# Two PSUM banks for the scores and four for everything else, with a new table of places

## What is computed

```python
# layer 0: group norm, 8 heads of 32 channels, projection, residual
h = group_norm(x) * gn_w + gn_b
q, k, v = split(qkv_w @ h + qkv_b)                  # per head 32 x 1024
w = softmax((q * scale).T @ (k * scale), axis=-1)   # 64 score matrices of 1024 x 1024
x = x + proj_w @ (w @ v) + proj_b
# layer 1: one head, queries and keys of 32 channels, values of 256, residual
energy = (Wq @ x).T @ (Wk @ x)
x = gamma * (softmax(energy) @ (Wv @ x)) + x
```

## Time and profile before

| | |
|---|---|
| median of 3 runs | 1619.43 us (1619.39 to 1620.1) |
| the profiled execution | 1615.41 us |
| its span, first to last instruction | 1613.5 us |
| TensorE busy | 1500.4 us, 93% |
| GpSimd (POOL) busy | 1199.0 us, 74% |
| VectorE (DVE) busy | 1132.3 us, 70% |
| ScalarE (ACT) busy | 752.1 us, 47% |
| mean granted TensorE clock | 0.954 |

### The profile page before, as it was taken

The page is one execution under the profiler, slowest core; times in us unless marked ns, Lnnn a source line. Parts: engine busy times, 40 slices in busy tenths (PEclk is TensorE's granted clock), DMA queues, the critical chain, the costliest instruction groups (busy, mean ns, idle before and its releaser), DMA issues.

```text
span 1613.5 us, 25511 instructions
## 1 busy us (share of the span) xinstructions
PE 1500.4 (93%) x7120; PEld 897.8 (56%) x7120; DVE 1132.3 (70%) x1916; ACT 752.1 (47%) x1377; POOL 1199.0 (74%) x560
## 2 busy tenths in 40 slices
PE   4889798999999999999999999999999999999968
PEld 1454354558545774558555674457555584556437
DVE  3776668877687677877688777877788777684243
ACT  2046354653546444653546445554546535563412
POOL 3069887895779777895889877796878958797804
PEclk9689889999999999999999999999999999999979
DMA  4040304030411214030220314020140304000100
GB/s 125 17 131 1 79 8 98 21 80 29 107 45 24 57 54 107 21 80 14 78 70 20 80 53 107 21 65 23 48 106 21 80 29 104 21 1 8 46 20 27
DMA packets 38741, 85.74 MB, mean 53 GB/s; under 512 B 10304, under 2 KB 20416, under 8 KB 38592
## 3 DMA queue, kind: packets, MB, share of 16 engines
q1 hardware_dynamic: 38208, 82.88, 20.5%
q0 software_dynamic: 384, 1.05, 0.3%
HBM read 18.29 MB, written 8.39 MB: 17 GB/s over the span
## 4 chain that ended last, share of the span: by engine, by line
PE 76%; DVE 9%; issue 7%; SPq 3%; ACT 2%; DMA 1%; POOL 1%; DVEq 0%; ACTq 0%; POOLq 0%
PE pv L516 14%; PE work L555 13%; PE st L485 13%; PE pv L494 11%; PE work L612 7%; DVE mpart L834 4%; PE work L575 4%; PE work L619 3%; PE work L587 3%; SPq L349 3%; PE work L581 2%; PE st L477 2%; PE work L561 2%; PE rec L533 1%; POOL acc L810 1%
## 5 line engine op out<-in xcount | busy, mean ns | idle before, releaser
L810 POOL TENSOR_TENSOR acc<-acc,probs 128x1024 f32<-128x1024 f32 x384 | 898.4, 2381 | 46.2 <-ACT probs L686 46.2
L686 ACT ACTIVATE probs<-st 128x512 f32<-128x512 f32 x1152 | 618.1, 602 | 480.0 <-PE st L485 375.4
L834 DVE TENSOR_REDUCE mpart<-work 128x1 f32<-128x512 f32 x1024 | 648.2, 681 | 184.2 <-PE work L555 180.8
L555 PE MATMUL work<-ks,qs 96*128 96x512 f32 x1024 | 428.2, 467 | 40.9 <-DVE vpd L880 14.5
L485 PE MATMUL st<-qs,ks 98*128 98x512 f32 x1024 | 404.4, 437 | 19.6 <-issue 17.2
L555 PEld LDWEIGHTS work<-ks,qs 96*128 96x128 f32 x1024 | 199.4, 198 | 203.0 <-DVE mpart L834 98.9
L810 POOL TENSOR_TENSOR acc<-probs 128x1024 f32<-128x1024 f32 x64 | 151.0, 2382 | 169.8 <-ACT probs L686 160.6
L485 PEld LDWEIGHTS st<-qs,ks 98*128 98x128 f32 x1024 | 197.4, 195 | 135.8 <-ACT probs L686 61.5
L494 PE MATMUL pv<-probs,vt 128*32 128x512 f32 x2048 | 252.5, 611 | 0.0
L516 PE MATMUL pv<-probs,l_vt 128*128 128x256 f32 x1024 | 235.7, 381 | 1.3 <-ACT raw L745 1.2
L516 PEld LDWEIGHTS pv<-probs,l_vt 128*128 128x128 f32 x1024 | 192.1, 190 | 35.6 <-ACT probs L686 5.0
(11 more groups left out here) (73 smaller groups left out, 967.3 us busy)
## 6 DMA issues: line engine op xcount, KB each, us to landing
qs<-part_hi SPq DMA_DIRECT2D x116, 128.0 KB, 2.6
ks<-part_hi SPq DMA_DIRECT2D x116, 128.0 KB, 2.4
xa<-in_x SPq DMA_DIRECT2D x16, 512.0 KB, 4.0
y<-in_x SPq DMA_DIRECT2D x8, 1024.0 KB, 5.4
out<-raw SPq DMA_DIRECT2D x32, 256.0 KB, 2.2
qs<-part_lo SPq DMA_DIRECT2D x60, 128.0 KB, 2.4
ks<-part_lo SPq DMA_DIRECT2D x60, 128.0 KB, 2.4
qs<-mrow SPq DMA_DIRECT2D x256, 2.0 KB
```

Of the source, the lines that this page charges most:

```text
L555: last = mm(bank, qs[g][0:HI_HI_LO, j, t0:t0 + P], ks[g][0:HI_HI_LO, j, half * HALF:(half + 1) * HALF], start=True, stop=True)
L686: nc.scalar.activation(probs[:, n % PRING, half * HALF:(half + 1) * HALF], st[:, (2 * n + half) % ST_BANKS, :], ACT.Exp).then_inc(s_exp1 i ...
L810: pool.tensor_tensor(a, first, probs[:, n % PRING, :], ALU.add).then_inc(s_add0, 1)
L834: last = dve.reduce_max(mpart[:, 4 * j + tb, half:half + 1], bank, AX.X)
```

## The change

One line gives one bank of the scores to the other pool, and the table of places is new in every row. What is computed, the number of entries of each kind and the piece of the program to which each belongs stay as they are. Of the table a few lines are shown:

```diff
-ST_BANKS, WORK_BANKS = 3, 3
+ST_BANKS, WORK_BANKS = 2, 4
...
-MAXIMA_OF_STOP = (2, 0, 0, 0, 3, 1, 0, 0, 3, 0, 1, 0, 2, 0, 1, 0, 4, 2, 0, 0, 2, 0, 1, 1, 0, 0, 0, 2, 0, 2, 1, 0, 1,
+MAXIMA_OF_STOP = (3, 0, 2, 0, 1, 3, 0, 2, 0, 1, 1, 3, 0, 1, 0, 0, 0, 0, 2, 2, 1, 1, 0, 0, 1, 0, 2, 0, 0, 0, 0, 0, 2,
...
-    "norm": (32, 33, 34, 40, 52, 53, 60, 72, 88, 112, 118, 119),
-    "sums": (9, 12, 14, 25, 25, 59, 61, 76, 95, 98, 126, 126, 149, 150, 150, 154, 155, 155, 157, 159),
+    "norm": (31, 31, 36, 38, 52, 53, 66, 86, 95, 116, 119, 121),
+    "sums": (12, 13, 13, 14, 23, 58, 63, 85, 95, 97, 134, 134, 135, 144, 148, 154, 154, 154, 154, 154),
```

More of the change, by code:

```diff
@@ L37 @@
 PIECE = HALF // PIECES
-MAXIMA_OF_STOP = (2, 0, 0, 0, 3, 1, 0, 0, 3, 0, 1, 0, 2, 0, 1, 0, 4, 2, 0, 0, 2, 0, 1, 1, 0, 0, 0, 2, 0, 2, 1, 0, 1,
[6 rows of a table removed]
-STEADY = {
-    "maxima1": (65, 68, 69, 70, 72, 77, 78, 84, 84, 90, 91, 93, 94, 107, 119, 120, 125, 134),
-    "qk1": (190, 205, 206, 208),
-    "norm": (32, 33, 34, 40, 52, 53, 60, 72, 88, 112, 118, 119),
-    "sums": (9, 12, 14, 25, 25, 59, 61, 76, 95, 98, 126, 126, 149, 150, 150, 154, 155, 155, 157, 159),
[L52 to L55, removed]
+MAXIMA_OF_STOP = (3, 0, 2, 0, 1, 3, 0, 2, 0, 1, 1, 3, 0, 1, 0, 0, 0, 0, 2, 2, 1, 1, 0, 0, 1, 0, 2, 0, 0, 0, 0, 0, 2,
[6 rows of a table added]
+STEADY = {
+    "maxima1": (63, 70, 71, 71, 74, 74, 79, 84, 85, 89, 89, 89, 95, 105, 119, 124, 131, 136),
+    "qk1": (190, 208, 208, 215),
+    "norm": (31, 31, 36, 38, 52, 53, 66, 86, 95, 116, 119, 121),
+    "sums": (12, 13, 13, 14, 23, 58, 63, 85, 95, 97, 134, 134, 135, 144, 148, 154, 154, 154, 154, 154),
+    "sums1": (156, 157, 160, 162, 162, 165, 168, 168, 168, 175, 180, 187),
+    "v0": (181, 190),
+    "layer1": (1, 23, 32, 37, 40, 50, 68, 98, 103, 145),
+    "v1": (8, 34),
     "maxima": [n for n, count in enumerate(MAXIMA_OF_STOP) for _ in range(count)],
```

## The result

The changed kernel takes **1670.58 us** (median of four runs, 1661.85 to 1674.05) against 1619.41 us (1612.61 to 1620.1) for the kernel before: ratio 1.0315, with a 95% interval of 1.028 to 1.0351. That is some 51 us slower, where 8.9 us were forecast and 1650 us was the upper end of the range.

A forecast was written before the change was run, and what follows sets the result against it. TensorE was taken to bound the loop. Six rounds x (4.3 - 1.3 - 1.6) = +8.4, -3.4 once for the clock, +2.9 and +1 gave +8.9 us; forecast 1628 us, range 1604 to 1650.

The forecast's parts named there:

- The direction: Whole kernel: slower by more than a measurement's 0.2% (3.2 us), with chances 0.40 + 0.10 + 0.06.
- The step that failed: Loop round: a walk asking how much TensorE work lies between each of 144 score fills and its bank's last fill.
- The branch: TensorE's 3.4 us issue gap at the loop's branch, which the change was said to leave alone.
- Scores, +4.3 a round: Loop round: score banks three to two, more fills waiting for exponentials, +4.3 us; bounds +1 and +11.5.
- Fourth work bank, -1.3 a round: Loop round: banks for other work three to four, less waiting for maxima, -1.3 us; bounds nothing and 1.4.
- G1, -1.6 a round: Loop round: TensorE's wait for `vpd`, the end of VectorE's G1, falls from 1.8 us to 0 to 0.2.
- Image 0, +2.9: `first`, at the empty slots: fourteen maxima instead of nine between sum and scores, four reductions more, +2.9 us.
- `last`, +1: `last`: +1 us for the scores of its first sixteen slots.
- The clock: Rival, loop: short score waits bring two half-clock stretches of 3.4 us each round, +20 us, 1648 us; chance 0.06.
- chains with ScalarE's other jobs: Rival, loop: ScalarE's part_hi and copies add to score waits, +8.4 us more a round, +54 us, 1673 us; chance 0.10.
- The signs: Loop round: over 18 loader waits for exponentials, about 10 us or more; no `vpd` wait; L834 waits halved from 9.3 us.
- marks for "wrong": Loop: rounds under 184 us; `vpd` or reciprocal waits left; exponential waits above 13 us with rounds above 190; clock under 0.97.

The follow-up runs named there:

- E10: Changed kernel with stack copies of two of four heads left out in loop and last image, 12 transfers instead of 24: 1639.16 us, ratio 1.0144.
- E2: Kernel before with its old table but the new banks, two for scores and four for other work: 1672.66 us, ratio 1.0346.
- E11: Kernel before with its old table, two score banks and three for other work: 1690.33 us, ratio 1.0457.
- E1: Changed kernel with the new table but the old banks, three for scores and three for other work: 1713.33 us, ratio 1.0602.
- E5: Kernel before with one entry moved, the first QK1 behind G1 from stop 47 to 41: 1605.68 us, ratio 0.9917.
- E3: Changed kernel with five maxima fills of stops 18 to 20 moved to stops 21 to 25: 1670.06 us, ratio 1.0328.
- E9: Kernel before with stack copies of two of four heads left out in loop and last image, 12 transfers instead of 24: 1613.09 us, ratio 0.9965.
- E6: Changed kernel with last three QK at stops 205, 206, 208 and maxima rows sent between the stack's `qs` and `ks` halves: 1700.86 us, ratio 1.0513.
- E7: Changed kernel with the last three QK of a round at stops 205, 206, 208 instead of 208, 208, 215: 1686.25 us, ratio 1.0425.

## Why the prediction was wrong, point by point

- **The direction** was right, and slower was given 0.56. The size was wrong: +51 us for +8.9.
- **The step that failed** is the sentence "TensorE's total work in a round is unchanged, so only waits count", followed by a walk that asked of each fill only how long ago its *bank* was used. The new table also sets when SyncE may begin its two stacks and the rows, and where their readers stand. The walk never went through that queue: 24 issues in 16.2 us, with 2.3 to 4.3 us until the last copy lands. Before, the stack landed 2.2 us ahead of its reader and the queue was free 1.3 us ahead of the rows; the table starts the stacks 2.3 and 5.5 us later in the round. The sum has no term for this, and it is the largest: the two waits are 3.8 us a round, 37.5 us of half clock lie at them, and with half of the copies left out (E10) half of the total loss is gone, or 32.5 of the loop's 46.8 us in the profiled executions. That the copies also land slowly in some rounds was not to be seen in a walk; it adds 1.5 to 1.9 us to the stack's wait where it happens, and its cause is open.
- **The branch** was said to stay as it is (3.4 us). It became shorter, 1.7 to 2.2 us, some 9 us in the loop to the good, which the sum lacks too.
- **Scores, +4.3 a round.** Right as far as the account tells: +2.5 in waits; the small delays grew by 1.9, as nineteen more late weight loads at 0.1 us would, though no run tells whose delays they are. Together 4.4. The walk had the old order's fills short by 11.5 us with two banks, the new order's by 4.1; the waits are 7.7 (E2) and 3.4. That the table at least halves this loss was right.
- **Fourth work bank, -1.3 a round.** Wrong in sign for bank and table together. The waits for VectorE other than `vpd` rose by 1.1. The bank itself is worth more than I said (3.5 us a round in the old order, E2 against E11, up to half of it clock), but the new table spends it on maxima in groups: with three banks it loses 14.4 us a round to VectorE in E1, with four 3.0. I counted reuse distances as if VectorE were always there at once, and in the groups it is not.
- **G1, -1.6 a round.** Right: `vpd` 1.8 to 0.3 us, and in E5 that one place alone is worth 14 us, the half clock included.
- **Image 0, +2.9.** The mechanism at the empty slots was right: GpSimd's gap is now

```profile
212.29 2.36 POOL L810 TENSOR_TENSOR acc<-probs 128x1024 f32<-128x1024 f32 x1 [17.92 <-ACT probs L686]
```

  17.9 us for 17.7 foretold. But `first` became longer by 8.5 us, not by 2.9. The same piece takes 166.4 us in E1 (only the table), 168.5 in E2 (only the banks), 161.2 in E3, and 158.3 to 161.7 in three kernels with the old table and three and three banks. Each half of the change makes it longer and both together no more than one. At half clock it spends 47.8 us instead of 41.0, which is 3.4 us of the 8.5 at most (E3, the shortest with the new table, has 33.3); which wait does the rest I did not isolate.
- **`last`, +1.** With the epilogue it was +5.8 us. In E10 it is 260.3 us against 258.0 in E9, so more than half of it goes with the copies that are left out.
- **The clock** rival foresaw two stretches of 3.4 us more at half clock in each round, from bursts of short score waits. In the loop 27.4 us more of half clock came, but not from there: E2, with 7.7 us of score waits a round, has 23.9 us of it, less than before, and all of it at the loop's branch. E11, with 7.9, has 44.4, at the branch and behind the wait for `vpd`. The new stretches of the changed kernel stand at the waits for transfers: in round 3, 655.5 behind the wait of 1.8 us that ends at 653.97, and 747.7 in the one of 2.4 us that ends at 748.48. The Trainium skill, in TensorE: Matmul & The Clock Gate, "A second HAM failure mode: psum-queue depth-cycling", describes the swing as coming from cycling through banks with small gaps; E2's 23.9 us and E11's 44.4 do not bear that out here, since none of it stands at the score waits. That the waits carry the clock with them is shown by E10, where both go. Why a stretch follows some such waits and not others stays open.
- **The rival "chains with ScalarE's other jobs"** gave 1673 us, 2 us from what was measured, and had 0.10. That is luck: it is +11.5 us a round of score costs, and the account has 2.5 in waits and at most 4.4. (Its +54 is also 3.4 us too much by the terms of the sum: 6 x 8.4 - 3.4 + 2.9 + 1 = +51.)
- **The signs.** Those for scores and `vpd` came (37 waits, 14.4 us; no wait for `vpd` in this round, though 0.6 us in rounds 5 and 6). The loader's waits for L834 fell from 9.3 to 5.1 us, not quite to half. Two marks for "wrong" came: waits for exponentials above 13 us with rounds above 190 (14.4 and 194.6), and a clock under 0.97 (0.96). The first points at the scores, which were not what the sum had wrong.

## What to carry to other kernels

When a table of places is changed, walk every queue that the table releases, the DMA issuer's too: when may it start, how many issues at how much each, when does the last land, and where does the reader stand now; a slack of 2 us can be all there is, and a landing can take 1.5 us longer in one round than in the next. A stretch in which one engine waits 2 us may cost more than 2 us, since the clock can fall behind it. And test the parts alone: here one moved entry (E5) held a gain of 14 us that the whole change buried.

## What the runs showed of the hardware

- A transfer of the stacks occupies SyncE's queue for about 0.6 us at issue (24 in 16.2 us); the two rows at L435 took 0.7 each. The rows landed 1.8 us behind the issue of the second in most rounds, 2.8 in two of the changed kernel's. The last copy of the keys landed 2.3 to 2.4 us behind its issue in most rounds of both kernels, and 3.8 to 4.3 us in four of twelve, for a reason that no run shows.
- The loop's branch: TensorE stood idle 3.2 to 3.9 us at it in the kernel before and 3.0 to 3.7 in E6 and E7, but 1.7 to 2.2 us in the changed kernel, where a QK stands at the last stop of the round.
- The price of a two-microsecond gap of TensorE: in E5, 1.6 us of wait a round, six times, is some 10 us, and the measured gain was 14 us; in E10, 3.5 us a round of transfer waits went together with 5.5 us a round at half clock, worth at most 2.7.
- A releaser in the chain of waits can be misnamed. At 745.8 it leads from L435 back to a maxima reduction of VectorE, although the rows were written at 743.66 and the queue had just issued its last key copy; the engine's own timeline told which it was.
